# Idle transposes on TensorE in the routing stage of a two-layer decoder

## The reference, cut to what matters

```python
x = inputs.reshape(b * s, e)
gate_logits = jnp.einsum('te,ex->tx', x, gate_kernel)
weights, selected = jax.lax.top_k(gate_logits, TOP_K)          # TOP_K = 2
weights = jax.nn.softmax(weights.astype(jnp.float32), axis=-1)
flat_experts = selected.reshape(-1)
sort_idx = jnp.argsort(flat_experts)
...
h0 = jax.lax.ragged_dot(sorted_x, w0, group_sizes)
h1 = jax.lax.ragged_dot(sorted_x, w1, group_sizes)
out_sorted = jax.lax.ragged_dot(jax.nn.silu(h0) * h1, wo, group_sizes)
```

## Time and profile before

| | |
|---|---|
| median of 3 runs | 5440.36 us (5432.55 to 5440.89) |
| the profiled execution's own time | 5445.14 us |
| its span, first to last instruction | 5443.4 us |
| mean granted TensorE clock | 0.977 |
| routing stage, first transposes to VectorE's last write | about 3430 to 3552 us |
| expert stage | about 3567 us to the end |

### The profile page before, as it was taken

How to read it: one execution, slowest core, us unless ns; L and a number is a source line. 1 busy time by engine, 2 the same in 40 slices (tenths; PEclk the granted TensorE clock), 3 DMA queues, 4 the chain that set the end, 5 groups by cost and what they waited for, 6 DMA issues and landing times. The chain is left out here.

```text
span 5443.4 us, 76081 instructions
## 1 busy us (share of the span) xinstructions
PE 5183.7 (95%) x25536; PEld 2577.0 (47%) x25536; DVE 2639.3 (48%) x4290; ACT 1644.7 (30%) x2110; POOL 1440.5 (26%) x1124
## 2 busy tenths in 40 slices
PE   9999989999999999899979999779999999999998
PEld 4444446644445444444444555634444444444444
DVE  4243237654443332254542566545555555555554
ACT  1011015522121100234321334124444444444343
POOL 1000015511122100000002222434444444444443
PEclk9999999999999999999999999789999999999999
DMA  1010021221011323599987112234456577789996
GB/s 57 8 54 0 16 76 52 78 81 33 21 31 62 107 93 125 137 218 211 218 191 246 39 63 74 97 109 116 147 178 207 159 247 246 254 281 335 382 383 236
DMA packets 492543, 771.57 MB, mean 142 GB/s; under 512 B 119153, under 2 KB 262262, under 8 KB 491844
## 3 DMA queue, kind: packets, MB, share of 16 engines
q1 hardware_dynamic: 376208, 723.32, 41.3%
q0 software_dynamic: 36160, 43.09, 4.0%
q10 hardware_dynamic: 79988, 2.67, 0.9%
HBM read 577.15 MB, written 116.26 MB: 127 GB/s over the span
## 5 line engine op out<-in xcount | busy, mean ns | idle before, releaser
L2978 PE MATMUL ex_ps<-ex_w,ex_xT 128*64 128x512 f32 x5248 | 1192.5, 596 | 15.4 <-DVE ex_w L2880 11.6
L2880 DVE COPY ex_w<-ex_shelf 128x4096 f32 x328 | 753.5, 2297 | 364.4 <-PE ex_ps L2978 232.7
L2929 ACT ACTIVATE ex_w<-ex_shelf 128x4096 f32 x164 | 593.4, 3618 | 883.9 <-PE ex_ps L2994 768.4
L2978 PEld LDWEIGHTS ex_ps<-ex_w,ex_xT 128*64 128x64 f32 x5248 | 366.3, 137 | 627.7 <-issue 588.8
L2994 PE MATMUL ex_ps<-ex_w,ex_hT 128*64 128x256 f32 x5248 | 596.4, 380 | 25.1 <-issue 21.2
L2826 POOL DMA_INDIRECT ex_x<-moe_xn,ex_ix x328 | 557.7, 1700 | 137.1 <-issue 99.1
L2843 POOL DMA_INDIRECT out<-ex_y,ex_ix_out x164 | 296.7, 1809 | 891.2 <-DVE ex_xT L2867 411.9
L2994 PEld LDWEIGHTS ex_ps<-ex_w,ex_hT 128*64 128x64 f32 x5248 | 383.2, 137 | 282.6 <-issue 119.8
L1561 PE MATMUL ff_ps<-ff_w,ff_hT 128*128 128x512 f32 x768 | 348.8, 597 | 5.2 <-DVE ff_w L1436 2.8
L1756 PE MATMUL pr_ps<-pr_w,pr_xT 128*128 128x512 f32 x768 | 334.5, 592 | 0.8 <-ACT pr_xT L225 0.8
L1510 ACT ACTIVATE ff_gT<-ff_ps,ff_bet,ff_gam 128x128 f32<-128x128 f32 x384 | 144.1, 459 | 458.8 <-PE ff_ps L1571 458.8
(11 more groups left out here) (300 smaller groups left out, 6836.3 us busy)
## 6 DMA issues: line engine op xcount, KB each, us to landing
ex_shelf<-L_ffn_w SPq DMA_DIRECT2D x128, 2048.0 KB
ex_shelf<-L_ffn_wo SPq DMA_DIRECT2D x64, 2048.0 KB
cv_gt<-cv_g SPq DMA_DIRECT2D x320, 128.0 KB
cv_vt<-cv_v SPq DMA_DIRECT2D x256, 128.0 KB, 4.6
ff_x<-x SPq DMA_DIRECT2D x16, 1024.0 KB
ex_raw_x<-slot_token ACTq DMA_DIRECT2D x656, 0.5 KB
at_low<-x SPq DMA_DIRECT2D x8, 1024.0 KB
x<-at_acc SPq DMA_DIRECT2D x8, 1024.0 KB, 4.2
```

The source lines that it names most:

```text
L2880: dve.tensor_copy(w_s[n][:, :], pick(shelf[n], buf)).then_inc(w_set[n].sem, 1)
L2929: act.activation(w_s[2][:, :], pick(shelf[2], buf), ACT.Copy).then_inc(w_set[2].sem, 1)
L2978: mm = pe.matmul(ps[q * G:(q + 1) * G, which, 0:FQ], xT[:, p % 2, k, :], wu[which][:, k, q * FQ:(q + 1) * FQ], start=k == 0, stop=k == KD - 1)
```

## The change

In each of the 8 passes of the chunk loop, 16 transposes of the identity into bank 2 are issued between logits(c+1) and ranks(c), and after the loop 32 more, ahead of the wait for the order's inputs. The program of the other engines is as it was (line numbers behind the change are two higher).

```diff
                 if c + 1 < NC:
                     turn(c + 1)
                     logits(c + 1)
+                turn_idle(pe, ps[:, 2], ident, 16)
                 ranks(c)
+            turn_idle(pe, ps[:, 2], ident, 32)
             pe.wait_ge(order_set, 2)
             row = ps[:, 5]
             pe.matmul(row[:, 0:NE], nt_b[:, :], upto[:, :], start=True, stop=True)
```

## The result

The changed kernel takes 5448.45 us (median of 20 runs, 5441.16 to 5454.14), the kernel before 5439.39 us on the same chip (20 runs, 5429.75 to 5448.89). The ratio is 1.0017, with a 95% interval from 1.0011 to 1.0024: 9.1 us slower (6 to 13), where +4.4 was forecast. That is inside the range and inside the 0.2% that I called no change, though the interval lies clear of 1.

What follows compares the result with a forecast made beforehand. At full clock a chunk was taken to be bound by scatter burst, late release and new slots (13.4 us), at half clock by TensorE. Terms 0.9 + 3.5 + 0 + 0 = +4.4 us on 5440.4 gave 5445 us, range 5431 to 5461.

Steps and rivals of the forecast that it cites:

- Price of one: Each added TensorE transpose was to cost 0.11 us at full clock and 0.22 us at half clock.
- Chunk 0: At full clock, 16 transposes delay the ranks, so slots and first scatter come later: +0.9 us.
- The hole and chunk 2: Transposes at half clock delay chunk 4's logits: +3.5 us, bounds 0 to +8.2; wrong if the hole differs from 11 us by over 3.
- Chunks 3 to 6: TensorE's 10.5 us a chunk stays below the 13.4 us scatter cycle; half-clock chunk -0.8 to +3.5 us; taken as 0.
- The end: The 32 transposes after the loop fit TensorE's 5.77 us idle before the order products: 0, bounds -1.3 to +1.2 us.
- the working theory: Full-clock chunk: scatter burst 10.0, TensorE's completions seen late 1.5, rank read and slots 1.9, together 13.4 us; at half clock TensorE bounds.
- Rule on gaps: Long gaps between matmul bursts drop the clock to half; alone it would shrink half-clock time by some 16 us; not summed.
- The rule against the change: Matmuls stay in program order, so filler is paid wherever `both` is ready; alone +12.6 us; not in the sum.
- TensorE as the bound at half clock (2): In chunks 3 to 6 a half-clock chunk takes 18.6 us against 13.4: +26 us, 5467 us; chance 0.15.
- the one of the clock that stays (4): The routing stage's mean clock stays near 0.72; times as in the first or second rival; no chance of its own.
- the late releases go (3): Late-seen completions vanish in the chunk loop and TensorE's 10.5 us set a chunk: -20 us, 5421 us; chance 0.10.
- "Everything is hidden" (1): The scatter cycle covers chunk 2 as well, so the change costs nothing: 5440 us; chance 0.25.

Runs made afterwards that it cites:

- the other chip: Both kernels rerun unchanged on a chip other than that of the first comparison: changed kernel 5413.92 us, ratio 0.9999; kernel before 5417.74 us, ratio 1.0005.
- e4_end_narrow: Kernel before with 16 products of one column added ahead of the order products: 5414.01 us, one time, against 5417.15 of before.
- e5_end_wide: Kernel before with 4 products of 512 columns added ahead of the order products: 5417.05 us, one time, against 5416.36 of before.
- e8_double: Changed kernel with 32 transposes in place of the 16 in each chunk: 5427.31 us, ratio 1.0015 to the kernel before.
- e3_land4: Kernel before, with GpSimd waiting ahead of each four scatters for the landing of the four before: 5444.06 us, ratio 1.0044.
- e10_before_half: Kernel before without the scatters of the second choices (32 of 64) and the waits for their landing: 5413.72 us, ratio 0.9991.
- e11_after_half: Changed kernel without the scatters of the second choices (32 of 64) and the waits for their landing: 5413.25 us, ratio 0.9991 to before.
- first chip: The chip of the first comparison, number unknown: changed kernel 5448.45 us against 5439.39 us before, ratio 1.0017.

## Why the prediction was half right

The sum was +4.4 us and the change cost 9.1 us: the total fell within the bounds, and two of the steps that make it up did not come about as told. By its steps:

- *Price of one:* right, 0.11 and 0.22 us.
- *Chunk 0:* +0.84 us measured, +0.9 forecast. Right.
- *The hole and chunk 2:* by its own test this step was wrong: the hole is not there any more. The interval of 20.1 us that held it and the 9.2 us ahead of it, between the `both` of successive chunks, became 15.4 and 14.6 us. The burst of chunk 2 comes only 1.4 us later than before (48.82 against 47.38 us), of which 0.84 is chunk 0. Forecast +3.5, measured +0.6. The total was within its bounds, the mechanism wasn't the one described. The reading that "the hole ends alike" was wrong in part: ScalarE's wait ended at 3472.66 because the transposes that it needs ran only then (fourteen of sixteen from 3471.98), behind TensorE's own stops. Late news of finished work explains VectorE's wait alone, whose logits had ended at 3460.94.
- *Chunks 3 to 6:* forecast 0, measured +1.3 us in the sum (+2.7 at the last burst, less 1.4). TensorE needs 10.1 us a chunk where it is the bound, forecast 10.5; on the other chip, with the scatters' cover of 10.1 us, that is nearly free. The bursts came 13.7, 14.5, 13.7 and 13.7 us apart (13 to 14 forecast).
- *The end:* this is the step that failed. I took 0, with bounds of -1.3 and +1.2, from the transposes' length and the clock alone. It cost 5.8 us. Both forecasts on TensorE held, the transposes fitted and the products ran at full clock, but their completion was seen 7 us late. I had the late release in the working theory and applied it only to the chunks. What makes these products late and not those of before is open. That they end while scatters are still going out isn't enough, since before's did too, 3.6 us ahead of the last scatter's end, and were seen at once. Nor are results held until a burst is over: `L2516` at 3476.84 went on in the middle of a burst (3470.35 to 3480.28), 2.7 us after its logits had ended.

  Two differences are left. One is the number of TensorE's instructions since the last two bursts, 0.95 us apart, began: 30 in before, over 60 in after. The other is the clock at which the products ran. Counting in both traces the results that ended while scatters ran and for which VectorE had to wait, the twelve made at full clock came 2.0 to 11.2 us late, and of the eight made at half clock six came at once and two 1.2 and 2.2 us late. (Some results that ended early in a burst were read without any wait.) That is a pattern in two traces, not shown by an experiment: the two runs built to part them, `e4_end_narrow` and `e5_end_wide`, met no late completion.
- *Rule on gaps* (the Trainium skill, "TensorE: Matmul & The Clock Gate", "Why this matters for your kernels"). The trace agrees that filler raises the clock, by 0.08 on both chips and 0.12 in the pair with half the scatters, but the 16 us that the rule alone would give back did not come. On the other chips the traces show why: TensorE didn't set the stage's end there. The rule against the change (same page, "Step-by-step: what each phase is for"), in-order work paid in full, holds where the cover is gone: in `e8_double` 1.8 us more of filler lengthened the chunk by 1.7 us.

Of the rivals, TensorE as the bound at half clock (2) fell: half-clock time in the stage went from 67 to 52 us. So did the one of the clock that stays (4): 0.72 became 0.80. That the late releases go (3) came about on the other chips, for both kernels alike and not through the change, and there TensorE's work sets a chunk of the changed kernel, as that rival said. "Everything is hidden" (1) is the result on the one other chip where both kernels ran; the two parts, each alone, gave the same on three more. A sum from the traces shows why. The experts begin some 10 us after the last scatter ends or some 13.6 us after VectorE's last write, whichever is later:

| | last scatter + 10.0 | last write + 13.6 | experts begin |
|---|---|---|---|
| before, other chip | 111.9 | 107.7 | 111.8 |
| after, other chip | 111.5 | 111.3 | 112.1 |
| `e3_land4` | 142.7 | 106.2 | 142.7 |
| `e8_double` | 122.2 | 124.1 | 124.2 |
| `e10_before_half` | 103.2 | 111.2 | 111.3 |
| `e11_after_half` | 105.0 | 111.9 | 111.8 |
| before, first chip | 132.4 | 135.4 | 136.6 |
| after, first chip | 135.1 | 143.9 | 143.9 |

(us from the stage's start; the two constants are read from `e3_land4` and `e10_before_half`, so those two rows fit by construction; the others fit within 0.6 us, but for before on the first chip, which is 1.2 us off.) On the other chip before had 4.2 us in hand on VectorE's side and the change uses 3.6 of them. On the first chip the late completions had used them up already, so every microsecond counts. They account for the difference between the chips: the experts begin 24.8 us later there than on the other (136.6 against 111.8), and before's medians are 5439.39 and 5415.65 us. Since nearly all runs in those medians were unprofiled, the late completions are most likely no matter of profiling, though no unprofiled run can show them. Their cause stays open, as no later trace had them. In both of the first chip's traces they come while scatters run; that the scatters cause them isn't shown, and can't be the whole of it, since on the other chips the same scatters run through and every reader is on time. A version that holds the order products until the scatters are out, or fewer scatters at the end, wasn't tried, since nothing on those chips could have shown its worth. So the 9.1 us on the first chip are placed in its trace, and why they arise isn't known. No version beat the kernel before by more than 0.1%.

## What to carry to other kernels

Filler on an in-order engine is paid as soon as another engine no longer sets the pace: count first how much that engine has in hand (here 4.2 us by the scatters' line), and then what the filler takes. A higher clock is worth nothing while TensorE isn't what the stage ends on. And a mechanism found in one part of a stage (a late release) has to be applied to every reader of that stage, above all to the one that closes it.

## What the runs showed of the hardware

- TensorE's completions can be seen late in one comparison and not in others, with the same program: 2 to 11 us late on the first chip, where the kernel takes 5439 us and TensorE also stops for up to 1.2 us at a time between products with no wait between them; on the five later ones at once and without stops, with 5415 to 5418 us.
- The clock fell to half in a stretch where TensorE had waited no longer than 0.74 us at a time (`e10_before_half`), and with the change's filler the stage's mean was 0.93 instead of 0.81 (`e11_after_half`).
- An indirect scatter issues every 1.26 us (0.96 and 0.30 between), and a wait for the landing of the last four left GpSimd idle for 1.9 to 3.9 us (`e3_land4`).
- The start of this stage, with nothing changed ahead of it, moves by up to 19 us between the profiled executions of kernels of 5.4 ms; two spans that agree to 0.2 us hid a difference of 8 us in the stage.
